# A gated cross-attention and expert layer on one core: a row maximum, an expert sum and an expert preparation change place, and TensorE's transposes become plain products

## The reference

```python
x = x + tanh(g_xattn[0]) * xattn(_layernorm(x), ctx_768, ...)   # ctx: 32 x 77 x 96
x = x + tanh(g_ffn[0]) * ffn(_layernorm(x), w_router, w1, w2)

# xattn: 16 heads of 8
xn, xfn = layer_norm(x, norm_g, norm_b), layer_norm(xf, tnorm_g, tnorm_b)
q, k, v = xn @ Wq + bq, xfn @ Wk + bk, xfn @ Wv + bv
w = softmax(einsum('bthd,bnhd->bhtn', q, k) / sqrt(8))
y = einsum('bhtn,bnhd->bthd', w, v)

# ffn: 8 experts, the two best of each token
top_vals, top_idx = top_k(x @ w_router, 2)
h = square(relu(einsum('nc,ecd->ned', xf, w1)))
y_all = einsum('ned,edc->nec', h, w2)
out = sum(take(y_all, top_idx) * softmax(top_vals))
```

## Time and profile before

| | |
|---|---|
| median of 3 runs | 371.83 us (370.3 to 375.83) |
| the profiled execution | 371.1 us |
| its span, first to last instruction | 369.3 us |
| mean granted TensorE clock | 0.897 |
| PE busy | 328.0 us, 2799 records |
| DVE busy | 237.8 us |
| ACT busy | 179.5 us |
| POOL busy | 105.9 us |

### The profile page before, as it was taken

The page is one execution under the profiler, slowest core; times in us unless marked ns, Lnnn a source line. Parts: engine busy times, 40 slices in busy tenths (PEclk is TensorE's granted clock), DMA queues, the critical chain, the costliest instruction groups (busy, mean ns, idle before and its releaser), DMA issues.

```text
span 369.3 us, 8185 instructions
## 1 busy us (share of the span) xinstructions
PE 328.0 (89%) x2799; PEld 249.4 (68%) x2799; DVE 237.8 (64%) x935; ACT 179.5 (49%) x408; POOL 105.9 (29%) x188
## 2 busy tenths in 40 slices
PE   0778978899999979998999899989998999799893
PEld 0435565567878757885778578857785888578672
DVE  5695777565657867586658666776766566524663
ACT  1332534544364636563565455555555455434552
POOL 6481515315103170226031623141312000200000
PEclk9996989955599989997999789998999899659999
DMA  3511401083505544474529271725183510250010
GB/s 90 147 40 32 124 2 48 21 126 70 195 39 91 81 140 164 74 100 126 177 45 129 53 249 37 117 59 200 51 115 52 202 46 4 65 196 2 1 30 28
DMA packets 18456, 32.95 MB, mean 89 GB/s; under 512 B 4905, under 2 KB 11530, under 8 KB 18416
## 3 DMA queue, kind: packets, MB, share of 16 engines
q1 hardware_dynamic: 14270, 24.45, 27.3%
q0 software_dynamic: 3296, 7.93, 9.0%
q10 hardware_dynamic: 850, 0.05, 0.2%
HBM read 21.04 MB, written 2.21 MB: 63 GB/s over the span
## 4 chain that ended last, share of the span: by engine, by line
PE 44%; DVE 6%; issue 2%; POOL 1%; ACT 1%; POOLq 0%; DVEq 0%
PE y L585 10%; PE c L532 6%; PE s L510 5%; PE h L576 4%; PE ab L488 3%; PE h L578 3%; PE h L577 3%; PE ab L556 2%; PE c L543 2%; PE ab L549 2%; PE ab L438 1%; DVE y_out L1075 1%; POOL rs L1226 1%; DVE y_out L1085 1%; PE y L602 1%
## 5 line engine op out<-in xcount | busy, mean ns | idle before, releaser
L941 DVE TENSOR_REDUCE negm<-ab 128x4 f32<-128x308 f32 x128 | 59.2, 476 | 51.3 <-PE ab L488 50.0
L775 ACT ACTIVATE p<-s 77x512 f32<-77x512 f32 x128 | 74.3, 584 | 26.6 <-PE s L510 26.4
L510 PEld LDWEIGHTS s<-qs,ks 104*77 104x77 f32 x512 | 61.4, 170 | 12.9 <-issue 7.4
L510 PE MATMUL s<-qs,ks 104*77 104x128 f32 x512 | 65.1, 256 | 1.3 <-ACT p L775 1.2
L585 PE MATMUL y<-w2s,hs 128*128 128x128 f32 x448 | 62.5, 284 | 0.3 <-ACT hs L782 0.3
L488 PE MATMUL ab<-ks,qs 96*128 96x312 f32 x128 | 54.3, 427 | 6.2 <-DVE negm L941 2.8
L585 PEld LDWEIGHTS y<-w2s,hs 128*128 128x128 f32 x448 | 57.5, 200 | 0.6 <-ACT hs L782 0.5
L532 PE MATMUL c<-p,vs 77*32 77x128 f32 x1024 | 53.3, 302 | 0.0
L782 ACT ACTIVATE hs<-u 128x512 f32<-128x512 f32 x56 | 35.1, 628 | 24.8 <-DVE u L1062 23.6
L1224 POOL TENSOR_SCALAR rs<-mv 128x1 f32<-128x1 f32 x32 | 8.4, 262 | 130.3 <-DVE mv L982 130.1
L1062 DVE SCALAR_TENSOR_TENSOR u<-h,gb 128x512 f32<-128x512 f32 x56 | 38.0, 679 | 6.2 <-DMA gb<-gates_scratch 4.2
(11 more groups left out here) (130 smaller groups left out, 512.3 us busy)
## 6 DMA issues: line engine op xcount, KB each, us to landing
gb<-gates_scratch SPq DMA_DIRECT2D x14, 768.0 KB, 5.7
gb<-gates_scratch SPq DMA_DIRECT2D x7, 512.0 KB, 4.5
qs<-q_hi SPq DMA_DIRECT2D x12, 256.0 KB, 5.5
ks<-k_hi SPq DMA_DIRECT2D x60, 39.0 KB
x_res<-in_x_dram POOLq DMA_DIRECT2D x8, 256.0 KB, 7.1
out_dram<-y_out POOLq DMA_DIRECT2D x8, 256.0 KB, 2.8
x_sb<-in_x_dram POOLq DMA_DIRECT2D x6, 256.0 KB, 5.3
qs<-q_lo SPq DMA_DIRECT2D x6, 256.0 KB, 7.7
```

The source lines that it names most:

```text
L510: mm = nc.tensor.matmul(p[0:N, T * i:T * i + T], ks[:, par, c, i, NP * j:NP * j + N], qs[:, par, c, T * j:T * j + T], start=True, stop=True)
L775: nc.scalar.activation(p32[:, c, :], src, ACT.Exp).then_inc(p_done, 1)
L941: nc.vector.tensor_reduce(negm[:, :, c], bank_ab[bank][:, 0:J * NP].rearrange("t (i n) -> t i n", n=NP)[:, :, 0:N], AX.X, ALU.max, negate= ...
```

## The change

1. DVE takes the first of the four row maxima of `near[3]` at the end of a slot, ahead of `normalise2`; it was the first instruction of the next slot, behind it.
2. `finish` and the store of a tile move from slot 1 to slot 2, on DVE between the second and the third row maximum; `x1` has three buffers instead of two.
3. `prepare_experts` leaves DVE (step 0, slot 1). ACT copies `w1_hi` and scales `w2s` in place in step -1, slot 2; POOL makes `w1_lo` in step 0, slot 0.
4. Every transpose of PE becomes a plain product with the identity: f32, and for `m_parts` fp32r with an identity `ident_r` that POOL makes at the start.
5. `keep_on` products: in each slot of step 0 three instead of two, in slots 0 and 1 of step 1 four instead of none.

```diff
+        ident_r = sb("ident_r", [128, 128], F32R)
...
-        w2_in = sb("w2_in", [D, E, D])
...
-        x1 = sb("x1", [T, 2, G, D])
+        x1 = sb("x1", [T, 3, G, D])
...
-                             (w2_in[:, :, :], w2.rearrange("e d c -> d e c")), (wr[:, :], w_router)):
+                             (w2s[:, :, :], w2.rearrange("e d c -> d e c")), (wr[:, :], w_router)):
...
                 for b in range(G):
-                    mm = nc.tensor.transpose(p[0:L, N * b:N * b + N], cn[:, b, :], ident[0:N, 0:N])
+                    mm = nc.tensor.matmul(p[0:L, N * b:N * b + N], cn[:, b, :], ident[0:N, 0:N], start=True, stop=True)
...
-                nc.tensor.transpose(p[0:SPLITS * H, 0:T],
-                                    m_parts[:, :, :, :].rearrange("t i a c -> t (i a c)").bitcast(F32),
-                                    ident[:, :]).then_inc(ready, 1)
+                nc.tensor.matmul(p[0:SPLITS * H, 0:T], m_parts[:, :, :, :].rearrange("t i a c -> t (i a c)"),
+                                 ident_r[:, :], start=True, stop=True).then_inc(ready, 1)
...
-                    mm = nc.tensor.transpose(bank_c[:, T * r:T * r + T], oT[:, T * r - 2 * T:T * r - T], ident[:, :])
+                    mm = nc.tensor.matmul(bank_c[:, T * r:T * r + T], oT[:, T * r - 2 * T:T * r - T], ident[:, :],
+                                          start=True, stop=True)
...
-                nc.tensor.transpose(p[:, 0:T], xn2[:, :], ident[:, :]).then_inc(ready, 1)
+                nc.tensor.matmul(p[:, 0:T], xn2[:, :], ident[:, :], start=True, stop=True).then_inc(ready, 1)
...
-                nc.tensor.transpose(bank_h[0][0:G * E, 0:T], gates[:, :, :].rearrange("t e b -> t (e b)"),
-                                    ident[:, :]).then_inc(gates_turned, 1)
+                nc.tensor.matmul(bank_h[0][0:G * E, 0:T], gates[:, :, :].rearrange("t e b -> t (e b)"),
+                                 ident[:, :], start=True, stop=True).then_inc(gates_turned, 1)
...
-                    if i == 0:
-                        keep_on(bank_h[0], 1)
+                    if i == 0 or (i == 1 and j < 2):
+                        keep_on(bank_h[0], 2)
...
-                    if i == 0:
-                        keep_on(bank_h[0], 1)
+                    if i == 0 or (i == 1 and j < 2):
+                        keep_on(bank_h[1], 2 if i else 1)
...
+            def prepare_experts():
+
+                act.wait_ge(experts_in, 16 * 3)
+                nc.scalar.activation(w1_hi[:, :, :], w1_in[:, :, :], ACT.Copy).then_inc(experts_made, 1)
+                act.wait_ge(tanh_done, 1)
+                nc.scalar.activation(w2s[:, :, :], w2s[:, :, :], ACT.Copy, scale=col(GF)).then_inc(experts_made, 1)
...
                     if near[2]:
                         max_store(*near[2])
+                    if (i, j) == (-1, 2):
+                        prepare_experts()
                     if near[0]:
                         exponent(*near[0], 2)
...
                 if j == 0:
                     dve.wait_ge(res_in[par], landed(s, par))
-                    if s >= 2:
-                        dve.wait_ge(y_added, s - 1)
+                    if s >= 3:
+                        dve.wait_ge(y_added, s - 2)
                 dve.wait_ge(post_d, at(POST, n, "scaled"))
-                nc.vector.tensor_tensor(x1[:, par, j, :].rearrange("t (i r e) -> t i r e", i=J, r=2),
+                nc.vector.tensor_tensor(x1[:, s % 3, j, :].rearrange("t (i r e) -> t i r e", i=J, r=2),
                                         x_res[:, par, j, :].rearrange("t (i r e) -> t i r e", i=J, r=2),
...
+            tops = {}
+
+            def tops_of(batch):
+
+                if batch not in tops:
+                    tops[batch] = maximum(*batch)
+                return tops[batch]
 
...
-            def prepare_experts():
-
-                dve.wait_ge(experts_in, 16 * 3)
-                nc.vector.tensor_copy(w1_hi[:, :, :], w1_in[:, :, :]).then_inc(experts_made, 1)
-                dve.wait_ge(tanh_done, 1)
-                nc.vector.tensor_scalar(w2s[:, :, :], w2_in[:, :, :], col(GF), None, ALU.mult)\
-                    .then_inc(experts_made, 1)
-                dve.wait_ge(experts_made, 1)
-                nc.vector.tensor_tensor(w1_lo[:, :, :], w1_in[:, :, :], w1_hi[:, :, :].bitcast(F32),
-                                        ALU.subtract).then_inc(experts_made, 1)
-
...
-                    top_scores = maximum(*near[2]) if near[2] else none
+                    top_scores = tops_of(near[2]) if near[2] else none
...
-                    if (i, j) == (0, 1):
-                        prepare_experts()
                     take(top_scores)
-                    take(top_scores)
+                    if j == 2 and exists(i - 2) and not last(i - 2):
+                        finish(i - 2, par)
                     take(top_scores)
                     if last(sf) and pending is not None:
...
                     take(gating)
-                    if j == 1 and exists(i - 2) and not last(i - 2):
-                        finish(sf, pf)
                     take(post)
...
                     take(prepare)
+                    if near[3]:
+                        take(tops_of(near[3]))
                     if near[-1]:
                         normalise2(*near[-1])
                     take(prepare, 9)
...
+            def low_experts():
+                pool.wait_ge(experts_made, 1)
+                nc.gpsimd.tensor_tensor(w1_lo[:, :, :], w1_in[:, :, :], w1_hi[:, :, :].bitcast(F32),
+                                        ALU.subtract).then_inc(experts_made, 1)
...
+            pool.wait_ge(const_made, 2)
+            nc.gpsimd.tensor_copy(ident_r[:, :], ident[:, :]).then_inc(const_made, 1)
...
                     if j == (2 if i == -1 else 0) and nxt:
                         load_rows(*nxt)
+                    if (i, j) == (0, 0):
+                        low_experts()
                     if near[-1]:
                         rstd(*near[-1])
...
-                    if j == 1 and exists(i - 2):
+                    if j == 2 and exists(i - 2):
                         store(i - 2, par)
```

12 lines of the change are left out of this document (6 added, 6 removed).

## The result

The changed kernel takes **384.05 us** (median of 4, 383.59 to 388.58) beside 373.83 of the kernel before in the same comparison: a ratio of 1.033, 95% interval 1.026 to 1.039. On a second chip it was 1.040 (1.033 to 1.047). Ratios and intervals here rest on undisturbed executions, medians on all; where too few were undisturbed, none is given. The page of the changed kernel, beside the earlier trace rows: busy time and clock, then the group of `u` and the first read of `gb`.

What follows compares the result with a forecast made beforehand. TensorE (PE), busy for 89% of 369.3 us, was taken as the bound. The terms 0.7 - 0.5 + 2.3 - 1.1 - 6.8 + 5.6 - 0.15 gave +0.05 on 371.1, so 371 us, range 360 to 380.

Steps and rivals of the forecast that it cites:

- The stall at L549: PE's wait after L562 for the turn of the normalised residual: 1.28 us of idling was to become 0.2.
- From L562 to L414: Five stretches from the gates' turn to the token turn: 41.7 to 36.6 us, gates' landing as bound; with two others, -6.8.
- The full-clock stretches are PE-bound and get +1.4 each: L414 to next L562: extra records of plain products lengthen each stretch by 1.4 us; the part's total +5.6.
- The sum assumes anyway: Stretches from L562 to L414: low clock was taken to go, counting 1.5 us of clock loss in the worked tile.
- slower, 381 us: Rival: 1.5 us of new idling before L414 makes the clock fall there, 1.5 to 3.1 us per fall; chance 0.11.
- A low clock costs 0.45 of each microsecond: Whole kernel: PE-bound work loses 0.45 us per microsecond at low clock, from L585 records of 1.10 against 2.02 us.
- The sum of steps 0 and 1: Up to 90.5 us: +2.3 for step 0's keep-ons and transposes, -1.1 for step 1, where a held clock returns time.
- Start: Up to 57 us: +0.7 for doubled x transposes, -0.5 for moved expert preparation and what goes with it.
- Behind the last L562: After 327 us: less low clock -1.5, transposes +0.9, late expert sum +0.45, together -0.15 us.
- Faster: Rival, 362.5 us: extra records hide under PE's waits, gates land in 3.7 us, step 1 gains 3; chance 0.34.
- Records without a return: Rival, 380 us: the clock falls where it fell, 9.4 us of clock gain goes, the records stay; chance 0.08.
- The stall stays: Case at L549: if the statistics do not move forward it starts at 131.0; 372 us, within the forecast, no own chance.

Runs made afterwards that it cites:

- e1: Changed kernel with all six kinds of TensorE transposes restored as true transposes: 367.7 us, ratio 0.986 to the kernel before.
- e2: Kernel before with plain products in place of its transposes, nothing else of the change: 394.3 us, ratio 1.057 to the kernel before.
- e18: e17 with all of TensorE's transposes as plain products: 378.9 us, ratio 1.016 to the kernel before.
- e17: e13 run again, beside e16: 360.6 us, ratio 0.968 to the kernel before.
- e7: Changed kernel with true transposes except the row maxima's plain fp32r product, and cn ahead of u: 364.4 us, ratio 0.962 to the kernel before.
- e13: e7 without the twelve added keep-on products: 361.0 us, ratio 0.973 to the kernel before.
- e16: e7 run again, on one chip with e17: 360.7 us, ratio 0.969 to the kernel before.
- e4: Changed kernel with the second half of cn ahead of the second u in slot 2 on VectorE: 374.5 us, ratio 1.009 to the kernel before.
- e5: Changed kernel with true transposes and cn ahead of u: 366.5 us, ratio 0.976 to the kernel before.
- e15: Changed kernel run again without any edit: 385.3 us, ratio 1.040 to the kernel before.
- e6: Kernel before with only the slot boundary's part (row maximum ahead of xn, expert sum and store in slot 2, three x1 buffers): 375.3 us, no ratio.
- e9: e7 with one more keep-on product behind L562 in slot 1 of steps that have experts: 364.5 us, ratio 0.973 to the kernel before.
- e12: Kernel before with only the change's twelve added keep-on products: 374.7 us, ratio 1.014 to the kernel before.
- e8: Kernel before with only the expert preparation moved to ScalarE and GpSimd: 366.0 us, ratio 0.978 to the kernel before.
- e10: e7 with plain products for the turns of the heads and the residual (L542, L549): 374.4 us, ratio 1.002 to the kernel before.
- e14: e8 with cn ahead of the second u: 368.4 us, no ratio given.
- e11: e7 with plain products for the turns of the normalised inputs (L414, L421): 371.0 us, no ratio given.

## Why the prediction was wrong

It gave 371 us, 360 to 380, and 0.19 to "slower"; the time is 384.

**The stall at L549: right.** 1.28 became 0.18 to 0.21. **From L562 to L414: right in size, for the predicted reason in three of five.** Predicted 36.6 for the five, measured 37.4. In three the gates are the bound and PE idles for 2.08, 1.35 and 1.26 us; in the other two (7.10 and 8.44) nothing waits at L414 and the length is that of a low clock, so there the size is luck; 283.73's stretch was to become 7.1 and is 7.3 (291.79 to the L585 at 299.06).

**"The full-clock stretches are PE-bound and get +1.4 each": mis-sized.** They get 1.8 to 2.0. The step that failed took 0.5 off the 1.9, for records that lie under the gates' wait or are given back. The plain products summed to about 12 us over the kernel; e1, e2 and e18 measure 16 to 18, and 20 to 23 at one clock. The bound that I kept, +9.5 for the five stretches, was where the value lay. Here the Trainium skill's Perfetto Trace Analysis, section Transposes, was right where I let part of the price hide: it tells to use true transposes for transpositions. The runs agree, with four records against eight and 18.3 us for the kernel (e18 beside e17).

**"The sum assumes anyway" that the low stretches go: wrong, and the main failure.** I let the fall of the clock hang on the 1.28 us of idling before L549. e7, e13 and e16 have 0.2 us of it and a low stretch of 6.8 us behind L562 in nearly every tile. A clock near 0.97 was named as the sign of being right; it was 0.934, and by the line above (an estimate) the 0.036 between them are 9 us of the 13 that were missed. In the changed kernel three tiles dropped behind L414 instead (33.3 in place of 31.7, so 1.6 each, 4.8 in all), and two in front of it, without any wait over 0.6 us near by (7.10 us at 0.76 and 8.44 at 0.60). The rival "slower, 381 us" named the first mechanism, its place and 1.5 us for a short fall, and had 0.11; its argument against, that 0.68 us of idling there did no harm before, did not carry to 1.35. e4 speaks for the wait as the cause: with `cn` ahead the wait at L414 and the three drops behind it are gone. Where the wait moved to L585, a drop followed it there in e5 (at 208.31, behind 2.08 us) and in e17 (at 137.02, behind 2.17). It is not the whole cause: e15 has a wait of 1.65 us at 184.29, e1 one of 1.33 and e6 one of 1.53 with the clock at 1.00 up to the next L562, e9 three of 1.8 to 2.6 before L584 without a drop, and the drops just behind L562 in e7 or e16 have no such wait in front. What brings those is open. Falls and records together are the miss of the middle: five stretches from L414 to L562 were to change by 5.3 us and changed by 163.2 - 151.6 = 11.6.

**"A low clock costs 0.45 of each microsecond": too much.** It was 0.33 over whole executions, and 0.2 to 0.35 for a fall just behind L562, which lies beside a wait. In step 1 I gave the clock 7.1 us less 2.4, that is 4.7; e7 and e16, one kernel, are 4.8 apart there, so the size was right, but e12 and e16 show that all of it went into the products. The sum of steps 0 and 1, +1.2, was near: from 57 us to the first L562 it is 34.3 after 33.5. But e1 has 30.95 there at the same clock, so that the plain products alone cost 3.3, and the preparation off VectorE gave more than I took.

**Start: near enough.** The first L562 moved by 0.8 us, predicted +1.4. That is in part luck: in e15, where the clock is low for 13.7 us in front of it, it moved by 4.1. The wait for ScalarE's copies before L488 was put at 1.4 and is 1.10 (at 31.95). The preparation alone (e8) is worth 2.5 us at one clock, predicted 1.4.

**Behind the last L562: wrong by 5 in the profile, by 2 in e15's.** Predicted nearly nothing, measured 55.3 for 50.4. The clock is low there for 19.4 us in place of 12.9, 6.5 more and some 3 us. In e15 it is 52.2 with 13.0 us at low clock, so that the long low stretch belongs to the one execution and not to the kernel; the 1.8 us that are left are records and the late sum, predicted +1.35. e12, which changes nothing behind step 1, has 54.0 us there, with a low stretch of 20.5 us that begins 1.6 us in front of it.

**The other rivals.** "Faster" (the extra records hide) is refuted: they cost 1.8 to 2.0 us in each full-clock stretch. "Records without a return" came near in time and not in its mechanism: the low stretches shrank from 76 to 50 us, and from 73.60 to the first L562 the clock was 1.00 in the profiled execution. "The stall stays" did not happen.

**The Trainium skill's rule on the clock** (TensorE: Matmul & The Clock Gate, Part 4: transpose mode does not count as busy in the same way): e2, with no transpose left, has a clock of 0.902 beside 0.892 of all executions of before, so the form alone did not lift it there; e10 and e18 are 0.02 above their partners, which their additional records could explain as well. The rule is neither shown nor refuted here. By it the plain form should lift the clock; whatever lifted it in e18 returned some 5 of 23 us.

The best kernels of the study are e16 and e17, 360.6 us, 3.2% under the kernel before: the change without its plain f32 products and with `cn` ahead of `u`, with the added keep-ons (e16) or without (e17).

## What to carry to other kernels

Ask of every wait that you remove which second chain ends beside it: here the stall at L549, the low clock and the gates' way through DRAM ran in parallel, and an edit that shortened one alone gained nothing (e6, e14), while two together gained up to 8 us. Where the bounding engine is busy for 98% of a stretch, price each record added to it in full and hide none of it. A higher granted clock is no gain by itself: read from stretches of equal work what it returned, and set that against what holds it. Before you put a low stretch down to an edit, look at a second trace of the same kernel: e7 and e16 are one kernel, with 17 us of low clock in step 1 and with none.

## What the runs showed of the hardware

- A plain f32 product of 128 x 128 has two records for a transpose's one and adds 0.14 us of PE time at full clock; the fp32r product of the row maxima has one record and takes 0.22 to 0.31 us at full clock (e7) where the transpose takes 0.27 (e5).
- The clock of one and the same kernel differs between executions: 0.851 to 0.923 for the kernel before, 16 us of time. Among the changed kernels it ran from 0.796 to 0.961.
- Low stretches began 0.2 to 3.3 us behind L562 in most tiles of most kernels, whether PE had idled 1.3 us there or 0.2, and often behind a wait of 1.3 us or more at L414 or L585. In e4, e9, e10 and e18 three tiles in a row went without.
- A low stretch just behind L562 cost 0.2 to 0.35 us for each of its microseconds (e11, e18), one that began 8 us later 0.48 (e9).
- With the same products in front, the clock from 57 us to the first L562 was 1.00 in e16 and 0.76 in e7.
